# A quantised two-layer graph kernel: scalar constants computed on GpSimd, one transposed tile copied by VectorE, the first adjacency split moved ahead

## What is computed

```python
h = relu(layernorm(x))
# layer 0
w_q     = quantise((weight - mean(weight)) / std(weight, ddof=1) / wgt_alpha)   # integers, -7 .. 7
h_q     = quantise(h / act_alpha)                                               # integers,  0 .. 15
support = relu(h_q @ w_q * act_delta * wgt_delta)
sup_q   = quantise(support / act_alpha2)                                        # integers,  0 .. 15
x = x + adj @ sup_q * support_delta
# layer 1
h = relu(layernorm(x))
x = x + attention_over_ones_of(adj) @ h
```

## Time and profile before

| what | value |
|---|---|
| three runs | 153.7, 154.11, 154.56 us (median 154.11) |
| the profiled execution | 155.06 us, of which the span from first to last instruction is 153.2 us |
| busy TensorE, share of the span | 137.9 us, 90% |
| busy VectorE, ScalarE, GpSimd | 109.0, 103.8, 33.3 us |
| mean share of full speed granted to TensorE | 0.986 |

### The profile page before, as it was taken

One profiled execution on the slowest core, in us unless ns is written; L12 is line 12 of the kernel. 1 busy time (PEld: TensorE's weight loads), 2 busy tenths in 40 slices (PEclk: granted clock), 3 DMA queues, 4 the chain that ended last, 5 costly groups with the idle time before them and its releaser, 6 DMA issues.

```text
span 153.2 us, 2115 instructions
## 1 busy us (share of the span) xinstructions
PE 137.9 (90%) x686; PEld 86.0 (56%) x686; DVE 109.0 (71%) x230; ACT 103.8 (68%) x154; POOL 33.3 (22%) x64
## 2 busy tenths in 40 slices
PE   0398999999998799999999999999999999999920
PEld 0394544555544355566665757475756666579910
DVE  0889888987964459996970696856869797765460
ACT  3688857498385759903982999999999788511000
POOL 2352044430303000008010101011010742711010
PEclk9999999999999999999999999999999999999995
DMA  5999998039949900070089999999211021011102
GB/s 156 365 416 420 400 391 321 4 63 281 274 118 265 103 0 0 0 274 4 0 218 361 281 340 370 379 366 344 85 71 65 3 73 68 0 68 68 68 4 77
DMA packets 12270, 27.45 MB, mean 179 GB/s; under 512 B 5088, under 2 KB 5344, under 8 KB 10592
## 3 DMA queue, kind: packets, MB, share of 16 engines
q1 hardware_dynamic: 11968, 26.88, 52.4%
q10 hardware_dynamic: 288, 0.39, 0.8%
HBM read 22.03 MB, written 4.19 MB: 171 GB/s over the span
## 4 chain that ended last, share of the span: by engine, by line
PE 64%; DVE 10%; DMA 8%; issue 6%; POOL 5%; ACT 3%; SPq 1%; POOLq 0%; DVEq 0%; ACTq 0%
PE acc L1049 26%; PE acc L1045 25%; DMA h_iT<-h_i 6%; PE acc L1029 4%; PE acc L1024 3%; POOL rs L578 3%; PE acc L1011 2%; DMA w_sb<-weight 2%; PE acc L1057 2%; DVE st L765 2%; DVE w_st L843 2%; ACT h_i L440 2%; PE acc L997 1%; DVE lo L815 1%; POOL nb L596 1%
## 5 line engine op out<-in xcount | busy, mean ns | idle before, releaser
L1049 PE MATMUL acc<-sup,lo 128*128 128x512 f32 (+1 forms) x208 | 48.3, 385 | 0.0
L1045 PE MATMUL acc<-sup_h,hi 128*128 128x512 f16 (+1 forms) x208 | 43.7, 364 | 0.0
L1049 PEld LDWEIGHTS acc<-sup,lo 128*128 128x128 f32 x208 | 37.1, 189 | 7.9
L563 POOL TENSOR_SCALAR nm<-mv 128x1 f32<-128x1 f32 (+2 forms) x19 | 12.9, 677 | 101.2 <-DVE ve L775 76.7
L421 ACT ACTIVATE junk<-raw,below 128x2048 uint8<-128x2048 f32 x16 | 31.8, 1989 | 0.0
L1045 PEld LDWEIGHTS acc<-sup_h,hi 128*128 128x128 f16 x208 | 19.4, 98 | 21.4 <-issue 2.9
L820 DVE TENSOR_TENSOR lo<-raw,hi 128x2048 fp32r<-128x2048 f32 x11 | 25.2, 2288 | 7.5 <-ACT hi L413 7.5
L455 ACT ACTIVATE ring<-x_sb,nm 128x512 f32<-128x512 f32 x15 | 10.4, 716 | 20.4 <-POOL nm L563 17.1
L1029 PE MATMUL acc<-sup,lo 128*128 128x512 f32 x64 | 22.0, 451 | 0.1
L413 ACT ACTIVATE hi<-raw 128x2048 f16<-128x2048 f32 x11 | 20.9, 1897 | 0.0
L765 DVE BATCH_NORM_STATS2 st<-x_sb 128x6 f32<-128x512 f32 x29 | 19.5, 688 | 0.4
(11 more groups left out here) (76 smaller groups left out, 83.7 us busy)
## 6 DMA issues: line engine op xcount, KB each, us to landing
raw<-adj_t SPq DMA_DIRECT2D x13, 1024.0 KB, 6.5
out<-ring SPq DMA_DIRECT2D x15, 256.0 KB, 5.7
x_sb<-x SPq DMA_DIRECT2D x3, 1024.0 KB, 13.8
raw<-adj_t SPq DMA_DIRECT2D x6, 512.0 KB, 4.9
w_sb<-weight SPq DMA_DIRECT2D x4, 258.0 KB, 4.0
x_sb<-x SPq DMA_DIRECT2D x1, 512.0 KB, 5.5
x_sb<-x ACTq DMA_DIRECT2D x1, 256.0 KB, 3.6
x_sb<-x SPq DMA_DIRECT2D x1, 256.0 KB, 4.6
```

The lines of the kernel that those rows point to most:

```text
L1045: nc.tensor.matmul(bank[:, cols], part(hi, k % PARTS, j), sup_h[:, j, cols], start=(j == 0), stop=False)
L1049: ins = nc.tensor.matmul(bank[:, cols], part(lo, k % PARTS, j), sup[:, j, cols], start=False, stop=(j == T - 1))
```

## The change

Six of VectorE's constant instructions (`constants`) and a seventh (`C_IQ` in `first_constants`) go; GpSimd computes the same seven: three ahead of `mean_of_sum(0)`, behind a wait for the first weight part, and four between `inverse_root(0, 1)` and `mean_of_sum(1)`. The semaphore `consts_ready` now counts four of them. ScalarE's `copy_T(1)` goes and VectorE runs `bound_hT(1)` behind the fourth `clip_w`. On ScalarE `split_piece(0)` moves ahead of `relu_sup(0)`. The warm-up behind the first transpose has 18 matmuls and not 20.

```diff
--- before.py
+++ after.py
@@ -51,7 +51,7 @@
     TURN = 8
     SLOTS = 4
 
-    WARM_SUMS, WARM_FIRST, WARM_T = 16, 4, (20, 0)
+    WARM_SUMS, WARM_FIRST, WARM_T = 16, 4, (18, 0)
     RAW = 7
     WHOLE = 4
     PARTS = 3
@@ -169,6 +169,7 @@
         w_rounded = sem("w_rounded")
         wq_ready = sem("wq_ready")
         qin_ready = sem("qin_ready")
+        const_part = sem("const_part")
         consts_ready = sem("consts_ready")
         x_summed = sem("x_summed")
         x_mean = sem("x_mean")
@@ -252,10 +253,10 @@
                 eng.wait_ge(h_ready, j - EARLY + 1)
 
         def wait_hT(eng, j):
-            if j < EARLY:
-                eng.wait_ge(hqT_ready, j + 1)
+            if j == 0:
+                eng.wait_ge(hqT_ready, 1)
             else:
-                eng.wait_ge(hqT_bounded, j - EARLY + 1)
+                eng.wait_ge(hqT_bounded, j)
 
 
         def wait_hi(eng, k):
@@ -478,9 +479,8 @@
             act.wait_ge(w_bias, 1)
             round_w(2)
             round_w(3)
-            copy_T(1)
+            split_piece(0)
             relu_sup(0)
-            split_piece(0)
             relu_sup(1)
             split_piece(1)
             round_h(2)
@@ -577,10 +577,31 @@
             def inverse_root(a, m):
                 nc.gpsimd.tensor_tensor(rs[:, a:a + m], ve[:, a:a + m], minus_half[:, 0:m], ALU.pow).then_inc(r_ready, 1)
 
+            def cc(i):
+                return cn[:, i:i + 1]
+
+            def scs(i):
+                return w_sb[:, 0, D + i:D + i + 1]
+
+
+            pool.wait_ge(w_in[0], 16)
+            nc.gpsimd.tensor_scalar(cc(C_IQ), scs(S_AA), 1.0 / ACT_LEVELS, None, ALU.mult).then_inc(const_part, 1)
+            nc.gpsimd.tensor_scalar(cc(C_SUP0), scs(S_AA), 1.0 / WGT_LEVELS, scs(S_WA), ALU.mult,
+                                    ALU.mult).then_inc(const_part, 1)
+            pool.wait_ge(const_part, 1)
+            nc.gpsimd.tensor_tensor(cc(C_IQ2), cc(C_IQ), cc(C_IQ), ALU.mult).then_inc(consts_ready, 1)
             pool.wait_ge(half_ready, 1)
             mean_of_sum(0)
             var_of_squares(0)
             inverse_root(0, 1)
+
+            nc.gpsimd.tensor_tensor(cc(C_OUT0), cc(C_RSC), scs(S_SCALE), ALU.mult).then_inc(const_part, 1)
+            nc.gpsimd.tensor_scalar(cc(C_W), cc(C_RWA), WGT_LEVELS, None, ALU.mult).then_inc(consts_ready, 1)
+            pool.wait_ge(const_part, 2)
+            nc.gpsimd.tensor_tensor(cc(C_SUP), cc(C_SUP0), cc(C_RAA2), ALU.mult).then_inc(consts_ready, 1)
+            pool.wait_ge(const_part, 3)
+            nc.gpsimd.tensor_scalar(cc(C_OUT), cc(C_OUT0), 1.0 / ACT_LEVELS, scs(S_AA2), ALU.mult,
+                                    ALU.mult).then_inc(consts_ready, 1)
             mean_of_sum(1)
             pool.wait_ge(w_var, 1)
             nc.gpsimd.tensor_tensor(ws(W_ROOT), ws(W_VAR), minus_half[:, 0:1], ALU.pow).then_inc(w_root, 1)
@@ -745,16 +766,6 @@
                 dve.wait_ge(w_in[0], 16)
                 chain(nc.vector.reciprocal(cn[:, C_RSC:C_RAA2 + 1], w_sb[:, 0, D:D + 4]))
                 nc.vector.tensor_scalar(cc(C_QIN), cc(C_RAA), ACT_LEVELS, None, ALU.mult).then_inc(qin_ready, 1)
-                nc.vector.tensor_scalar(cc(C_IQ), scs(S_AA), 1.0 / ACT_LEVELS, None, ALU.mult)
-
-            def constants():
-                nc.vector.tensor_scalar(cc(C_W), cc(C_RWA), WGT_LEVELS, None, ALU.mult)
-                nc.vector.scalar_tensor_tensor(cc(C_SUP0), scs(S_AA), 1.0 / WGT_LEVELS, scs(S_WA), ALU.mult, ALU.mult)
-                nc.vector.tensor_tensor(cc(C_IQ2), cc(C_IQ), cc(C_IQ), ALU.mult)
-                chain(nc.vector.tensor_tensor(cc(C_OUT0), cc(C_RSC), scs(S_SCALE), ALU.mult))
-                nc.vector.tensor_tensor(cc(C_SUP), cc(C_SUP0), cc(C_RAA2), ALU.mult)
-                nc.vector.scalar_tensor_tensor(cc(C_OUT), cc(C_OUT0), 1.0 / ACT_LEVELS, scs(S_AA2), ALU.mult,
-                                               ALU.mult).then_inc(consts_ready, 1)
 
             def wait_x(t):
                 for n, (a, m) in enumerate(x_loads):
@@ -799,8 +810,9 @@
                 else:
                     dve.wait_ge(h_turned[j % 2], 16 * ((j - TURN) // 2 + 1))
                     turned = h_iT[:, j % 2, :, :].rearrange("p k i -> p (k i)")
-
-                dve.wait_ge(sup_in_psum, j - 1)
+                if j >= 2:
+
+                    dve.wait_ge(sup_in_psum, j - 1)
                 nc.vector.tensor_scalar(h_qT[:, j % 2, :], turned, 0.0, ACT_LEVELS, ALU.max, ALU.min).then_inc(hqT_bounded, 1)
 
             def quantise_sup(i):
@@ -856,7 +868,6 @@
             first_constants()
             chain(w_stats(1))
             nc.vector.bn_aggr(w_half[:, :], w_st[:, 0:KD // 2, :].rearrange("p k s -> p (k s)")).then_inc(w_sum, 1)
-            constants()
             w_stats(2)
             after = step(w_stats(3))
             dve.wait_ge(w_tot, 1)
@@ -877,7 +888,7 @@
             stats(2)
             dve.wait_ge(w_root, 1)
             dve.wait_ge(dve_chain, after)
-            dve.wait_ge(consts_ready, 1)
+            dve.wait_ge(consts_ready, 4)
             W = D * D
             chain(nc.vector.tensor_scalar(ws(W_SCALE), ws(W_ROOT), cc(C_W), ((W - 1.0) / W)**0.5, ALU.mult, ALU.mult))
             nc.vector.scalar_tensor_tensor(ws(W_BIAS), ws(W_SCALE), -1.0, ws(W_MEAN), ALU.mult, ALU.mult).then_inc(w_bias, 1)
@@ -889,6 +900,7 @@
             for k in range(KD // 2, KD):
                 dve.wait_ge(w_rounded, k - KD // 2 + 1)
                 clip_w(k)
+            bound_hT(1)
             normalise(3, stats(3))
             quantise_sup(0)
             lo_of_piece(0)
```

## The result

| | us |
|---|---|
| changed kernel, median of 22 runs | 154.81 (153.34 to 156.48) |
| kernel before, 22 runs beside it | 153.97 (153.24 to 154.91) |
| ratio | 1.0044, 95% interval 1.0023 to 1.0066 |
| profiled execution of the changed kernel | 155.02, span 153.2 (before: 155.06, span 153.2) |

The change makes the kernel 0.44% slower, where 0.35 us less was forecast; 154.81 lies 0.11 us above the range given. The medians and ranges are of all runs, while every ratio in this text leaves out the runs more than 1.5% above the fastest of their kernel, so that a ratio need not be the quotient of two medians. The first thing to see is that the two profiled executions are equally long while the medians differ by 0.84 us: the runs spread over 1.7 us for the kernel before and 3.1 us for the changed one, so one pair of profiles can show where things moved but not what they are worth.

The account below looks back on a forecast made before the run. TensorE alone bounds the kernel from 60.64 us; before it, loops through several engines. 0.28 us left at `sup_h` plus 0.06 from the split make 0.35 us sooner: median 154.11 less 0.35, 153.8 us, range 153.1 to 154.7.

Parts of the forecast that it names:

- The bound and the place: TensorE alone sets the pace from 60.64 us; the change can pay only by letting that stretch begin sooner.
- The local steps up to 17 us: Start of the kernel: second sum gains 0.40 us, 0.28 to 0.30 left at `sup_h`, first loop 0.35 us sooner.
- the GpSimd rival: Four constants at 0.59 us each delay tile 1 and the weight's root: 0.6 to 0.9 us slower, 155.0 us, chance 0.07.
- the order of ScalarE and the copy on VectorE: Before `lo` of piece 1: copy costs VectorE 0.34 us, leaving 0.28 to 0.30 of 0.40; earlier split gains 0.06.
- whatever starts the first loop sooner should move every later one by as much: Loops before 60.64 us have no fixed date, so the 0.35 us gained at the start reaches TensorE's long stretch.
- The whole 0.54 us is there, with nothing to spare: VectorE's weight statistics start 0.54 us sooner; the fourth, at 6.53 us, falls just behind its load's landing.
- The clock: Rival: TensorE still at 1.2 GHz when the first support comes; slower or no gain, 154.1 to 155.5 us, chance 0.11.
- the cover that the prediction had counted on: First support's fourth matmul needs the fourth clip only at about 12.9 us, hiding ScalarE's smaller gain; without it 0.2 us remain.
- The rivals: Besides the forecast (0.50): gain dulled, about 154.1 us, 0.20; more than the sum, 153.2, 0.12; GpSimd 0.07; clock 0.11.

Follow-up runs that it names:

- the 36: 36 more warm-up matmuls ahead of TensorE's first weight sum, in four kernels: before 1.0021, changed 1.0013, changed plus one ScalarE instruction 1.0002, before with only constants moved 0.9983.
- the one delayed by twenty waits: Changed kernel with twenty already satisfied waits ahead of ScalarE's first sums: 156.73 us, ratio 1.0199 against the kernel before.
- the order alone: Kernel before with tile 1's transposed copy on VectorE and `split_piece(0)` ahead of `relu_sup(0)`, constants and warm-up as before: 154.36 us, ratio 1.0024.
- the order alone with ScalarE +1: Kernel before with the same two order edits and one more ScalarE instruction, from waits ahead of tile 1's sum: 154.30 us, ratio 1.0042.

## Why the prediction was wrong

- **The bound and the place: right.** The second phase is untouched, and only the date at which it begins matters.
- **The local steps up to 17 us: right to 0.25 us.** Third statistic 6.04 (forecast 5.9), second sum 8.18 (8.2), weight root 9.36 (9.35), mean of tile 1 8.65 (8.4), squares 8.89 (8.67), ScalarE's first rounding 10.79 (10.6), transposes of tile 1 at 11.75 (11.75), `sup_h` 14.01 (14.0), first `hi` 14.36 (14.3). The gain of 0.35 us at the `lo` of piece 1 measured 0.37. Constants cost 0.19 to 0.27 us, and the one beside the wide VectorE operation 0.52: there the Trainium skill (SBUF — State Buffer, "SBUF: two separate sides") was right that the two engines hold each other up. The root still came at 9.36, so the GpSimd rival did not happen; but tile 1's path behind the constants lost what was forecast for ScalarE's rounding, 0.02 us sooner and not 0.21, and the chain now runs there.
- **The step that failed first: the order of ScalarE and the copy on VectorE, summed as a gain of 0.06 less a loss of about 0.1.** Measured alone it costs 0.24%, 0.42% with ScalarE's instruction put back (an interval that leaves out 1), and 0.6% when the constants are moved as well: up to 1 us where the sum had 0.05. The constants without it lie at 0.9974 to 0.9988 in four measurements, on the forecast's side; every kernel with it lies above 1. Why it costs that much stays open. Up to tile 8's transpose its profile has no loss: the first `hi` matmuls come 0.4 us sooner and the transpose 0.1 us sooner, both counted from the first weight statistic. ScalarE's fetch, back in its place at 0.42%, is not what it hangs on.
- **The step that failed next: "whatever starts the first loop sooner should move every later one by as much".** It has no price for the stage that follows. The 0.37 us are whole at 30.9 us and gone by 61 us. Between lie eight transposing DMAs of 2.4 to 6.7 us, which the sum held at no cost and no variation, and whose stretch lasts 28.3 to 30.2 us over the profiles of this study. What the runs do not show is a fixed date: a start 1.45 us late cost some 1.3 us. So a shift is passed on in the main, with a spread several times the 0.35 us.
- **"The whole 0.54 us is there, with nothing to spare": half right.** There was nothing to spare, and no price was put on that. In 5 of 14 profiles VectorE waited for a weight part; the mean gain at the second sum is 0.11 us and not 0.40. With the constants on VectorE the same loads hid behind them.
- **The clock: the slow matmuls of the rival are there, its reason is not shown.** Eight matmuls of the first supports took 2.04 to 2.27 us (1.89 before) in four profiles without the 36, all of kernels with the constants moved, and 0.43 us each in the one delayed by twenty waits. But these are not all sooner supports: two of the four started at 12.45 and 12.98 us, against 12.52 in the kernel before. The clock's rise moved by itself: in the kernel before, the order alone and the order alone with ScalarE +1, whose TensorE programs are the same up to there, the 20 warm-up matmuls behind the first transpose took 2.34, 1.93 and 1.35 us, and the granted clock rose at 12.5, 11.0 and 10.0 us. The Trainium skill (TensorE: Matmul & The Clock Gate, Part 1) says that the rise varies by half a microsecond between executions; these traces show 2.5 us. An earlier warm-up went with 0.31% less in the changed kernel twice, for reasons that are not the clock of the supports alone: there the eight took 2.18 us at the fast level, since the first support now came before the last clip (12.24 us), the cover that the prediction had counted on.
- **The range** was built on a median of three runs with 0.3 us for noise. The rivals were weighed as exclusive cases, though several small ones can hold at once; waits for loads, slow matmuls and long transposes of some tenths each were all seen. That made the upper end too low.

What stays open: how the order of two engines costs 0.2 to 0.6%, and how the 0.44% divides between it, the clock and the fetches, since most parts are below 0.35% and near their interval's width.

## What to carry over

A sooner start is worth what is left of it after the next stage with a variable length; look for that stage (here eight transposing DMAs) and compare its spread over several executions with the gain. Work that stands ahead of the use of a load also hides that load's jitter: price the move by the late landings and not by the median one. Test the parts of a change one at a time and together: here one part was on the fast side and another undid it. And look where instruction fetches fall: one instruction more or less on ScalarE moved one of its fetches by 4 us. Whether a gain or loss of the median comes from that was not shown here.

## What the hardware showed unexpectedly

- Transposing DMAs take longer when a fetch of instructions falls beside them: 4.1 us became 5.9 and 6.0 with TensorE's fetch beside tile 9's, 4.7 to 4.9 in four of five profiles with ScalarE's there (4.2 in the changed kernel's own), and 2.4 became 4.1 us with TensorE's where no load ran. The Trainium skill (Runtime: NRT & Kernel Launch, "Instruction fetch mechanics") has instructions come in blocks of 256 by the sequencer's own DMA queue, at a cost "mostly hidden"; the queues are in these traces, and beside a transpose that an engine waits for the cost was not hidden.
- One ScalarE instruction less moved q14's packet from between 31.2 and 32.8 us to between 34.5 and 36.4; put back it undid this, and seven further ones moved it no more.
- Kernels with the same TensorE program had its clock rise at 10.0, 11.0 and 12.5 us.
- A wait ahead of the first activation puts the table load of 1.28 us behind that wait: the first sums came 1.5 us late (5.81 against 4.32).
- A GpSimd product on one column takes 0.19 to 0.32 us, and 0.52 us when it starts together with a 128x512 VectorE operation; the root takes 0.57 us and more.
